# First attention of a two-layer decoder block: transposed scores computed by a second product, with the row maximum as two rows of the operand stacks

## The chip, the cores and the metric

One core of a Trainium2 chip runs the whole program. The metric is the device time of one execution in microseconds. An engine here is TensorE (PE; PEld is its weight load), VectorE (DVE), ScalarE (ACT), GpSimd (POOL) or SyncE (SP), which only issues transfers.

## The reference

Two layers of gated cross attention and feed-forward over x of 4 x 512 tokens x 512, all in float32. Only the first attention concerns the change:

```python
q = _qdq(x) @ _qdq(wq).T + bq            # 16 heads of 32
k, v = jnp.split(cond @ wkv.T + bkv, 2, axis=-1)
attn = softmax(einsum('bnhd,bmhd->bhnm', q, k) * 32 ** -0.5, axis=-1)   # 512 x 512 per head
o = einsum('bhnm,bmhd->bnhd', attn, v).reshape(B, N, C)
```

4 batches of 16 heads make 64 heads of 512 queries by 512 keys. Its output o goes through an int8 step, a projection and the first mixture of experts; the second layer follows. These stages are the same in both kernels.

## The kernel before

The program is a row of stages, each with a block per engine, and the engines meet between stages. `l0_projections` (L207) writes q, k and v of the first attention to DRAM as high and low halves: a float32 number is the sum of two numbers that TensorE's float32r products keep, so a product of two such numbers is a sum of products of halves. `l0_attention` (L671) is the stage of the change, `l0_output` (L981) follows it.

**Units.** 16 groups of 4 heads (`NG`, `HG0`), each head 4 tiles of 128 queries (`QT`): `N` = 256 tiles. SP loads a group's stacks: `Qs` holds for each head the rows q high, q high, q low, q low (4 x 32 = 128 rows), `Ks` k high, low, high, low, so that one product over 128 rows is the full product of the halves. Eight loads fill them (`load_stacks`, L731). `V` holds the values' halves side by side (64 columns a head) and between each two heads a block of zeros.

**Per tile.** `scores` (L850 to L860) is one product of 512 columns into one of three banks `pS`. `maxima` (DVE, L933) takes the negated maximum over 512 keys. `exps` (ACT, L903) writes exp(score - max) to `Pr` in SBUF and sums the row (`rowsum`). `transposes` (L862) turns the 128 x 512 tile by four TensorE transposes into one of three banks `pT`. `high` (ACT, L913) copies that bank to `PTh` as high halves, `low` (DVE, L940) subtracts to get the low halves `PTl`; both read PSUM. `values` (L870) multiplies: for each of the 4 key tiles of a head two products of 512 queries, high and low, into `pO`. Two heads share `pO`, each in its own 64 rows; this is what the zeros in `V` are for.

**Per pair of heads.** `o_copy` (ACT, L921) copies `pO` to SBUF, `o_transposes` (L887) turns it back by four transposes into `pR`, and `normalise` (DVE, L947 to L964) takes the reciprocals of the row sums, adds the two halves of v and multiplies. SP stores a group's output (L769).

**Order.** Each engine runs a list written by hand, in order. `pipeline` (L40) calls, for each step, the functions of an engine in the order of its list, each for the item that lies its lag behind: in TensorE's list `(values, 9)` works on the tile nine steps back. Engines meet through semaphores: `Flag.done(n)` is the value that says item n is done, `past(n, k)` that item n - k is, `free(n)` is `past(n, 2)` and `part(n, k)` speaks of part k of an item.

```python
pipeline(pe, N, 2 * UN, [(transposes, 3), (scores, 0), (values, 9), (o_transposes, 10)])
pipeline(act, N, 2 * UN, [(high, 3), (exps, 1), (o_copy, 9)])
pipeline(dve, N, 2 * UN, [(low, 4), (maxima, 0), (normalise, 10)])
```

**POOL** has no part in the attention itself. Once per group (L822 to L844) it waits for the group's scores and then issues a store of zeros to `rows` in DRAM (16 in all), at group 1 the loads of constants and weights for the next stage (`load_constants`, L3528, and `load_weights`, L805), at groups 2 to 5 `split_weights` (L812): a high and a low half of a weight tile of 896 columns and of one of 512, and at group 6 two small scalings.

## Time and profile before

| what | us |
|---|---|
| median of 3 runs (lowest, highest) | 3174.27 (3173.81, 3181.19) |
| the profiled execution | 3173.65 |
| its span, first to last instruction | 3171.9 |
| busy TensorE, weight loads | 2922.6, 2362.8 |
| busy VectorE, ScalarE, POOL | 2342.8, 2088.9, 1369.7 |

A busy time is the sum of an engine's instructions over the span; instructions of one engine can overlap a little, so their durations can be longer than the distance between their starts. "Idle before" is the time that an engine stood still just ahead of an instruction, with what ended it. An engine waits for its own list only: idle time on an engine that is not the one the others wait for costs nothing. The names of tiles carry the stage's letter: b_ is the first attention, a_ the projections before it, c_ the stage after it, and h_ is the second layer's attention.

### The profile page before, as it was taken

How to read it: one execution, taken by the hardware profiler on the slowest of the kernel's cores; microseconds unless marked ns; L12 is line 12 of the kernel's file. 1: busy time of each engine (PE TensorE's matmuls, PEld its weight loads, DVE VectorE, ACT ScalarE, POOL GpSimd, SP SyncE). 2: the span in 40 equal slices, each digit the busy share in tenths (PEclk: the TensorE clock that was granted, in tenths of full speed). 3: DMA queues.
4: the chain of work that ended last, by engine and by line, in shares of the span. 5: the costliest groups of instructions: out<-in, count | busy, mean ns of one | idle time of the engine just before them, and what ended most of it. 6: DMA issues, size and time to landing. Idle time of an engine off the chain costs nothing. (4 is left out here: it accounts for less than half of the span.)

```text
span 3171.9 us, 56528 instructions
## 1 busy us (share of the span) xinstructions
PE 2922.6 (92%) x15414; PEld 2362.8 (74%) x15414; DVE 2342.8 (74%) x4695; ACT 2088.9 (66%) x4262; POOL 1369.7 (43%) x1701
## 2 busy tenths in 40 slices
PE   6878997887999999789999899999999999899888
PEld 5656665676888877578878688888888888688754
DVE  5679998765777668866666189988989888734377
ACT  4478987422666546466666488888888888633265
POOL 4412000413001076166666277777777777441132
PEclk9989999898999999989999999999999999999999
DMA  6897663216888589756566523322322332296400
GB/s 205 268 225 170 150 163 101 87 39 232 290 262 285 167 290 256 197 158 182 152 187 197 187 67 98 98 75 95 96 85 84 98 96 72 71 305 198 138 35 34
DMA packets 427166, 491.09 MB, mean 155 GB/s; under 512 B 53044, under 2 KB 284372, under 8 KB 426996
## 3 DMA queue, kind: packets, MB, share of 16 engines
q1 hardware_dynamic: 414036, 436.50, 46.2%
q0 software_dynamic: 12960, 52.61, 4.8%
q8 instruction: 72, 1.18, 0.2%
q14 instruction: 98, 0.80, 0.1%
HBM read 312.69 MB, written 176.31 MB: 154 GB/s over the span
## 5 line engine op out<-in xcount | busy, mean ns | idle before, releaser
L2806 POOL TENSOR_SCALAR h_probs<-h_exp,h_rowsum_inv 128x512 f32<-128x512 f32 x512 | 356.2, 696 | 278.8 <-PE h_pT L2654 262.9
L2734 DVE TENSOR_REDUCE h_neg_max<-h_scores 128x1 f32<-128x512 f32 x512 | 349.0, 682 | 144.6 <-PE h_scores L2646 144.4
L2696 ACT ACTIVATE h_exp<-h_scores,h_neg_max 128x512 f32<-128x512 f32 x512 | 355.0, 693 | 110.7 <-DVE h_neg_max L2734 100.5
L2747 DVE TENSOR_TENSOR h_probsT_lo<-h_pT,h_probsT_hi 128x512 fp32r<-128x512 f32 x512 | 347.8, 679 | 0.0
L2654 PEld LDWEIGHTS h_pT<-ident,h_probs 128*128 128x128 f32 x2048 | 255.7, 141 | 71.5 <-POOL h_probs L2806 1.8
L2654 PE MATMUL h_pT<-ident,h_probs 128*128 128x128 f32 x2048 | 307.4, 272 | 1.0 <-POOL h_probs L2806 0.8
L2705 ACT CAST h_probsT_hi<-h_pT 128x512 fp32r<-128x512 f32 x512 | 300.6, 587 | 0.9 <-PE h_pT L2654 0.9
L2922 PE MATMUL k_acc<-k_w_hi,k_cat 128*128 128x512 f32 x512 | 201.2, 393 | 11.4 <-POOL k_w_lo L3003 10.5
L2669 PE MATMUL h_pO<-h_probsT_hi,n_lo 128*128 128x512 f32 x512 | 203.3, 397 | 0.0
L2923 PE MATMUL k_acc<-k_w_lo,k_cat 128*128 128x512 f32 x512 | 200.7, 392 | 0.0
L910 ACT ACTIVATE b_probs<-b_scores,b_neg_max 128x512 f32<-128x512 f32 x256 | 179.8, 702 | 24.4 <-DVE b_neg_max L937 24.4
L937 DVE TENSOR_REDUCE b_neg_max<-b_scores 128x1 f32<-128x512 f32 x256 | 173.3, 677 | 20.8 <-PE b_scores L859 20.8
L2908 ACT CAST k_cat<-k_cat 128x512 fp32r<-128x512 bf16 x128 | 79.2, 621 | 160.5 <-PE k_acc L2923 141.7
L2505 DVE TENSOR_TENSOR g_normed<-g_pQ,g_rstd 128x512 f32<-128x512 f32 x160 | 110.2, 689 | 99.6 <-PE g_pT L2410 97.1
L2535 POOL TENSOR_TENSOR g_rstd<-g_var_eps,neg_half 128x4 f32<-128x4 f32 x160 | 171.7, 1073 | 13.4 <-POOL g_var_eps L2533 0.2
L919 ACT CAST b_probsT_hi<-b_pT 128x512 fp32r<-128x512 f32 x256 | 151.3, 591 | 34.9 <-PE b_pT L867 34.9
L944 DVE TENSOR_TENSOR b_probsT_lo<-b_pT,b_probsT_hi 128x512 fp32r<-128x512 f32 x256 | 173.4, 678 | 0.6
L867 PE MATMUL b_pT<-ident,b_probs 128*128 128x128 f32 x1024 | 162.6, 282 | 9.6 <-DVE b_probsT_lo L944 8.0
L2793 POOL TENSOR_TENSOR n_lo<-n_raw,n_hi_second 128x512 fp32r<-128x512 f32 x128 | 165.0, 1289 | 0.0
L867 PEld LDWEIGHTS b_pT<-ident,b_probs 128*128 128x128 f32 x1024 | 116.5, 142 | 64.8 <-ACT b_probs L910 46.8
L2454 ACT ACTIVATE g_out<-g_pT,head_ln_b,head_ln_w 128x512 f32<-128x512 f32 x160 | 124.4, 778 | 57.5 <-DMA lnT<-g_out 56.9
L2400 PE MATMUL g_pQ<-g_w_hi,n_hi_second 128*128 (+1 forms) x320 | 134.2, 419 | 24.5 <-POOL g_w_lo L2518 24.5
(453 smaller groups left out, 9006.7 us busy)
## 6 DMA issues: line engine op xcount, KB each, us to landing
e_w_raw<-in_w SPq DMA_DIRECT2D x24, 1792.0 KB, 8.0
lnT<-g_out SPq DMA_DIRECT2D x160, 256.0 KB, 2.4
n_raw<-lnT SPq DMA_DIRECT2D x64, 512.0 KB
e_w_raw<-in_w SPq DMA_DIRECT2D x24, 896.0 KB, 9.7
n_raw<-lnT SPq DMA_DIRECT2D x64, 256.0 KB
n_raw<-v SPq DMA_DIRECT2D x64, 256.0 KB
cat<-h_cat SPq DMA_DIRECT2D x128, 128.0 KB, 1.8
k_cat<-cat SPq DMA_DIRECT2D x128, 128.0 KB, 4.7
```

The costliest lines, as they stand in the source:

```text
L867: last = nc.tensor.transpose(pT[r % TB][:, k], Pr[:, r % 4, bass.ts(k, P)], g["ident"][:])
L910: nc.scalar.activation(Pr[:, r % 4], pS[r % SB][:], ACT.Exp, bias=nmax[:, r % 4:r % 4 + 1], accum_out=rsum[:, gb * HG0 + h, q:q + 1]).then ...
L944: nc.vector.tensor_tensor(PTl[:, h, :, bass.ts(q, P)], pT[r % TB][:], PTh[:, h, :, bass.ts(q, P)], ALU.subtract).then_inc(lo_done.sem, 1)
L2654: last = nc.tensor.transpose(pT[r % 4][:, k], Pn[:, r % 4, bass.ts(k, P)], g["ident"][:])
L2669: nc.tensor.matmul(pO[h][:], vl, PTh[:, br * HPG + h, k], start=False, stop=(k == QT - 1)).then_inc(o_mm.sem, 1)
L2696: nc.scalar.activation(Pr[:, r % 4], pS[r % 2][:], ACT.Exp, bias=nmax[:, r % 4:r % 4 + 1], accum_out=rsum[:, r % 4:r % 4 + 1]).then_inc(ex ...
L2705: nc.scalar.copy(PTh[:, br * HPG + h, :, bass.ts(q, P)], pT[r % 4][:]).then_inc(hi_done.sem, 1)
L2734: v.tensor_reduce(nmax[:, r % 4:r % 4 + 1], pS[r % 2][:], axis=AX, op=ALU.max, negate=True).then_inc(nmax_done.sem, 1)
L2747: v.tensor_tensor(PTl[:, br * HPG + h, :, bass.ts(q, P)], pT[r % 4][:], PTh[:, br * HPG + h, :, bass.ts(q, P)], ALU.subtract).then_inc(lo_ ...
L2806: nc.gpsimd.tensor_scalar(Pn[:, r % 4], Pr[:, r % 4], rinv[:, r % 4:r % 4 + 1], 1.0, ALU.mult, ALU.mult).then_inc(norm_done.sem, 1)
L2922: nc.tensor.matmul(bank[:], lhsT, Wh[:, k], start=(k == 0), stop=False)
L2923: ins = nc.tensor.matmul(bank[:], lhsT, Wl[:, k], start=False, stop=(k == CK - 1))
```

## The change

All of it is in `l0_attention`. The unit of the lists becomes a head (`NH` = 64), its work is done in two halves of two tiles (`HALF`).

- The score product now has 96 rows (low times low is left out; six loads). It serves the maximum alone: `pS` is one buffer of two banks, and VectorE takes the maxima of two query tiles in one instruction of 2 x 512 columns.
- POOL splits the four columns of negated maxima into high and low and puts them into columns 96 and 97 of `Mx` (zeros elsewhere). `max_rows` multiplies each by an identity, which yields the maxima as two rows on partitions 96 and 97 of `pMR`; ScalarE copies them under the query stack (`max_copy`). The key stack has ones in rows 96 and 97.
- `scores_t` computes the scores a second time with keys as rows: the stacks of 98 rows give score minus maximum, transposed. ScalarE's exponential of 2 x 512 columns writes the transposed probabilities to `Pr`; there are no transposes of tiles.
- The halves are made from `Pr` in SBUF: key tiles 0 and 1 high on VectorE (`high_a`) and low on POOL (`low_a`); key tiles 2 and 3 high on ScalarE (`high_b`) and low on VectorE (`low_b`). On odd heads POOL takes key tile 2 of these low halves (`low_c`).
- `V` has 65 columns a head, the last one of ones, so row 64 of `pO` is the row sum. `o_rows` multiplies 65 rows by `fold`, which adds the value halves and turns the result, per head, 33 columns for each of four query tiles. Its target `pR` is part of the bank `pMR`. `normalise` is a reciprocal of the sum column and a multiplication over 4 x 32 columns.
- POOL's side work hangs on its list: one of 64 smaller zero stores per head, the weight split one instruction a head in heads 8 to 23, the loads at head 4. POOL's list has no loop.

The diff, cut to its core (a line of "..." marks what is left out):

```diff
-    UN = HG0 * QT
-    PAIRS = HG0 // 2
-    V_LOADS = ((0, 0, 1), (2, 1, 2), (5, 3, 1))
+    HALF = QT // 2
     NG = B * H0 // HG0
-    SB, TB = 3, 3
-    N = NG * UN
+    NH = NG * HG0
+    ROUND_TRIP = 2 * HG0
+    STACK = 3 * DH0
+    DEEP = STACK + 2
+    OW = 2 * DH0 + 1
...
-        V = m.sb("v", [P, 2, QT, 3 * PAIRS, 2 * DH0], F32R)
-        Pr = m.sb("probs", [P, 4, S])
+        V = m.sb("v", [P, 2, QT, HG0, OW], F32R)
+        Pr = m.sb("probsT", [P, 2, QT, S])
...
-        pS = [m.ps(f"scores{j}", [P, S]) for j in range(SB)]
-        pT = [m.ps(f"pT{j}", [P, QT, P]) for j in range(TB)]
+        nmax = m.sb("neg_max", [P, 2, QT])
+        Mx = m.sb("max_columns", [P, 2, QT, DEEP], F32R)
+        ident_r = m.sb("ident_r", [P, P], F32R)
+        fold = m.sb("fold_parts", [OW, DH0 + 1])
+        rinv = m.sb("rowsum_inv", [P, 2, QT])
+        pS = m.ps("scores", [P, HALF, S])
+        pST = [m.ps(f"scoresT{j}", [P, HALF, S]) for j in range(2)]
         pO = m.ps("pO", [P, S])
-        pR = m.ps("pR", [P, QT, P])
+        pMR = m.ps("pMR", [P, S])
+        pR = pMR[:, 0:QT * (DH0 + 1)].rearrange("p (k c) -> p k c", k=QT)
...
-        QK_LOADS = 8
-        ZR = ROWS // NG
...
+        QK_LOADS = 6
+        ZR = ROWS // NH
...
-                for w, stack, parts in ((0, Qs, (0, 0, 1, 1)), (1, Ks, (0, 1, 0, 1))):
+                for w, stack, parts in ((0, Qs, (0, 0, 1)), (1, Ks, (0, 1, 0))):
...
-                wait(sp, s_done.sem, s_done.depth + (n - 1) * UN)
+                wait(sp, st_done.sem, (st_done.depth + (n - 1) * HG0) * HALF)
...
-                wait(sp, o_mm.sem, o_mm.depth + (n - 1) * UN)
-                for slot, head, heads in V_LOADS:
-                    sp.dma_start(V[:, r, :, slot:slot + heads].rearrange("p k s c -> p k (s c)").bitcast(F32),
-                                 t["v0"][bass.ds(tok, S), bass.ds(ch * 2 + head * 2 * DH0, heads * 2 * DH0)]
+                wait(sp, o_mm.sem, o_mm.depth + (n - 1) * HG0)
+                for h in range(HG0):
+                    sp.dma_start(V[:, r, :, h, 0:2 * DH0].bitcast(F32),
+                                 t["v0"][bass.ds(tok, S), bass.ds(ch * 2 + h * 2 * DH0, 2 * DH0)]
                                  .rearrange("(k p) c -> p k c", p=P)).then_inc(v_in[r], 16)
...
-            for b in range(2):
-                nc.gpsimd.memset(V[:, b, :, 1::3].bitcast(F32), 0.0).then_inc(v_zeroed, 1)
+            nc.gpsimd.memset(Mx[:].bitcast(F32), 0.0).then_inc(cleared, 1)
+            nc.gpsimd.memset(V[:, :, :, :, 2 * DH0:OW].bitcast(F32), 1.0).then_inc(prepared, 1)
+            nc.gpsimd.tensor_copy(ident_r[:], g["ident"][:]).then_inc(prepared, 1)
...
-            for k in range(NG):
-                pool.wait_ge(s_done.sem, s_done.depth + max(k * UN, UN // 2))
-                pool.dma_start(rows[k * ZR * D:(k + 1) * ZR * D].rearrange("(p a) -> p a", p=P), Z[:]).then_inc(z_out, 16)
-                if k == 1:
+            def split_weights(k, step):
+                if step == 0:
...
+                k, h = divmod(n, HG0)
+                pool.dma_start(rows[n * ZR * D:(n + 1) * ZR * D].rearrange("(p a) -> p a", p=P), Z[:]).then_inc(z_out, 16)
+                if k == 1 and h == 0:
...
-                    split_weights(k - 2)
-                    if k < KT:
+                    split_weights(k - 2, h)
+                    if k < KT and h == HG0 - 1:
                         load_weights(k)
...
+                pool.wait_ge(nmax_done.sem, nmax_done.done(n))
+                pool.wait_ge(mrow_mm.sem, mrow_mm.free(n))
+                nc.gpsimd.tensor_copy(Mx[:, r % 2, :, STACK], nmax[:, r % 2]).then_inc(mx_hi.sem, 1)
+                pool.wait_ge(mx_hi.sem, mx_hi.done(n))
+                nc.gpsimd.tensor_tensor(Mx[:, r % 2, :, STACK + 1], nmax[:, r % 2], Mx[:, r % 2, :, STACK],
+                                        ALU.subtract).then_inc(mx_done.sem, 1)
+
...
+                pool.wait_ge(hi_a.sem, hi_a.done(n))
+                nc.gpsimd.tensor_tensor(PTl[:, h, 0:HALF], Pr[:, r % 2, 0:HALF], PTh[:, h, 0:HALF],
+                                        ALU.subtract).then_inc(lo_a.sem, 1)
...
+                if third(r):
+                    pool.wait_ge(hi_b.sem, hi_b.done(n))
+                    nc.gpsimd.tensor_tensor(PTl[:, h, HALF], Pr[:, r % 2, HALF], PTh[:, h, HALF],
+                                            ALU.subtract).then_inc(lo_c.sem, 1)
+                if isinstance(n, int):
+                    beside(n)
+
+            pipeline(pool, NH, ROUND_TRIP, [(max_columns, 1), (low_a, 2), (low_c, 2)], NH)
...
+                    pe.wait_ge(nmax_done.sem, nmax_done.part(n - 1, 1))
+                else:
+                    pe.wait_ge(nmax_done.sem, nmax_done.part(n, 0))
+                for j in range(HALF):
+                    last = nc.tensor.matmul(pS[:, j], Qs[0:STACK, gb, h, bass.ts(half * HALF + j, P)], Ks[0:STACK, gb, h],
+                                            start=True, stop=True)
+                last.then_inc(s_done.sem, 1)
...
+                pe.wait_ge(mx_done.sem, mx_done.done(n))
+                pe.wait_ge(o_done.sem, o_done.past(n, 4))
+                for q in range(QT):
+                    last = nc.tensor.matmul(pMR[0:DEEP, bass.ts(q, P)], Mx[:, r % 2, q], ident_r[:], start=True, stop=True)
...
+                if half == 0:
+                    pe.wait_ge(mrow_done.sem, mrow_done.done(n))
+                pe.wait_ge(exp_done.sem, exp_done.part(n - 1, half))
+                for j in range(HALF):
+                    last = nc.tensor.matmul(pST[half][:, j], Ks[0:DEEP, gb, h, bass.ts(half * HALF + j, P)],
+                                            Qs[0:DEEP, gb, h], start=True, stop=True)
+                last.then_inc(st_done.sem, 1)
...
+                    pe.wait_ge(lo_a.sem, lo_a.done(n))
+                    pe.wait_ge(oT_done.sem, oT_done.past(n, 1))
+                    if h == 0:
+                        pe.wait_ge(v_in[gb], (i + 1) * 16 * HG0)
+                else:
+                    pe.wait_ge(lo_b.sem, lo_b.done(n))
+                    if third(r):
+                        pe.wait_ge(lo_c.sem, lo_c.done(i * HG0 + r // 2))
+                for k in range(half * HALF, (half + 1) * HALF):
+                    nc.tensor.matmul(pO[0:OW], V[:, gb, k, h], PTh[:, h, k], start=(k == 0), stop=False)
+                    last = nc.tensor.matmul(pO[0:OW], V[:, gb, k, h], PTl[:, h, k], start=False, stop=(k == QT - 1))
+                if half == 1:
+                    last.then_inc(o_mm.sem, 1)
...
+                pe.wait_ge(o_done.sem, o_done.past(n, 1))
...
-                    last = nc.tensor.transpose(pR[:, k], Os[:, pair_buffer(r), bass.ts(k, P)],
-                                               g["ident"][:])
+                    last = nc.tensor.matmul(pR[:, k], Os[0:OW, r % 2, bass.ts(k, P)], fold[:], start=True, stop=True)
...
-            pipeline(pe, N, 2 * UN, [(transposes, 3), (scores, 0), (values, 9), (o_transposes, 10)])
...
+            pipeline(pe, NH, ROUND_TRIP, [(half_of(scores, 0), 0), (max_rows, 1), (half_of(values, 0), 3),
+                                          (half_of(scores_t, 0), 1), (half_of(scores, 1), 0), (half_of(values, 1), 3),
+                                          (half_of(scores_t, 1), 1), (o_rows, 4)])
...
-                nc.scalar.activation(Pr[:, r % 4], pS[r % SB][:], ACT.Exp, bias=nmax[:, r % 4:r % 4 + 1],
-                                     accum_out=rsum[:, gb * HG0 + h, q:q + 1]).then_inc(exp_done.sem, 1)
...
-                nc.scalar.copy(PTh[:, h, :, bass.ts(q, P)], pT[r % TB][:]).then_inc(hi_done.sem, 1)
...
+                act.wait_ge(mrow_mm.sem, mrow_mm.done(n))
+                nc.scalar.copy(Qs[STACK:DEEP, gb, h], pMR[STACK:DEEP]).then_inc(mrow_done.sem, 1)
...
+                n, gb, h = head(i, r)
+                act.wait_ge(st_done.sem, st_done.part(n, half))
+                if half == 0:
+                    act.wait_ge(lo_a.sem, lo_a.free(n))
+                else:
+                    act.wait_ge(lo_b.sem, lo_b.free(n))
+                    if third(r):
+                        act.wait_ge(lo_c.sem, lo_c.past(i * HG0 + r // 2, 1))
+                nc.scalar.activation(Pr[:, r % 2, half * HALF:(half + 1) * HALF], pST[half][:], ACT.Exp).then_inc(exp_done.sem, 1)
...
+                act.wait_ge(exp_done.sem, exp_done.part(n, 1))
+                act.wait_ge(o_mm.sem, o_mm.past(n, 4))
+                nc.scalar.copy(PTh[:, h, HALF:], Pr[:, r % 2, HALF:]).then_inc(hi_b.sem, 1)
...
-            pipeline(act, N, 2 * UN, [(high, 3), (exps, 1), (o_copy, 9)])
+                act.wait_ge(oTr_done.sem, oTr_done.free(n))
+                nc.scalar.copy(Os[0:OW, r % 2], pO[0:OW]).then_inc(oT_done.sem, 1)
+
+            pipeline(act, NH, ROUND_TRIP, [(max_copy, 1), (high_b, 2), (lambda i, r: exps(i, r, 0), 1), (o_copy, 3),
+                                           (lambda i, r: exps(i, r, 1), 1)])
...
+                dve.wait_ge(s_done.sem, s_done.part(n, half))
+                if half == 0:
+                    dve.wait_ge(mx_done.sem, mx_done.free(n))
+                nc.vector.tensor_reduce(nmax[:, r % 2, half * HALF:(half + 1) * HALF], pS[:], axis=AX, op=ALU.max,
...
-                nc.vector.tensor_tensor(PTl[:, h, :, bass.ts(q, P)], pT[r % TB][:],
-                                        PTh[:, h, :, bass.ts(q, P)], ALU.subtract).then_inc(lo_done.sem, 1)
...
+                dve.wait_ge(exp_done.sem, exp_done.part(n, 0))
+                dve.wait_ge(o_mm.sem, o_mm.past(n, 4))
+                nc.vector.tensor_copy(PTh[:, h, 0:HALF], Pr[:, r % 2, 0:HALF]).then_inc(hi_a.sem, 1)
...
+                dve.wait_ge(hi_b.sem, hi_b.done(n))
+                k = HALF + 1 if third(r) else HALF
+                nc.vector.tensor_tensor(PTl[:, h, k:], Pr[:, r % 2, k:], PTh[:, h, k:], ALU.subtract).then_inc(lo_b.sem, 1)
...
+                dve.wait_ge(oTr_done.sem, oTr_done.done(n))
+                dve.wait_ge(o_done.sem, o_done.free(n))
+                nc.vector.reciprocal(rinv[:, r % 2], pR[:, :, DH0]).then_inc(rinv_done.sem, 1)
+                dve.wait_ge(rinv_done.sem, rinv_done.done(n))
...
+                nc.vector.tensor_tensor(O[:, gb, :, h * DH0:(h + 1) * DH0], pR[:, :, 0:DH0],
+                                        rinv[:, r % 2].unsqueeze(2).to_broadcast([P, QT, DH0]), ALU.mult).then_inc(o_done.sem, 1)
...
+            nc.vector.memset(Ks[STACK:DEEP].bitcast(F32), 1.0).then_inc(prepared, 1)
...
-            pipeline(dve, N, 2 * UN, [(low, 4), (maxima, 0), (normalise, 10)])
...
+            pipeline(dve, NH, ROUND_TRIP, [(normalise, 5), (lambda i, r: maxima(i, r, 0), 0), (low_b, 2),
+                                           (lambda i, r: maxima(i, r, 1), 0), (high_a, 1)])
```

## Rows read from the trace of the kernel before

**Rows 1.** Windows view, the attention: busy us (count) of PE, PEld, DVE, ACT, POOL; clock; DMA

```profile
167.00:543.00 376.00, 331.55 (x1920) 250.16 (x1920) 348.42 (x608) 323.37 (x800) 38.05 (x47) 0.98 0.67 161
```

**Rows 2.** Groups of instructions, 157 to 543 us: count, busy us, mean ns, idle before, releasers

```profile
L910 ACT ACTIVATE b_probs<-b_scores,b_neg_max 128x512 f32<-128x512 f32 x256 | 179.8, 702 | 24.4 <-DVE b_neg_max L937 24.4
L944 DVE TENSOR_TENSOR b_probsT_lo<-b_pT,b_probsT_hi 128x512 fp32r<-128x512 f32 x256 | 173.4, 678 | 0.6
L937 DVE TENSOR_REDUCE b_neg_max<-b_scores 128x1 f32<-128x512 f32 x256 | 173.3, 677 | 20.8 <-PE b_scores L859 20.8
L867 PE MATMUL b_pT<-ident,b_probs 128*128 128x128 f32 x1024 | 162.6, 282 | 9.6 <-DVE b_probsT_lo L944 8.0 <-ACT b_probs L910 1.3
L919 ACT CAST b_probsT_hi<-b_pT 128x512 fp32r<-128x512 f32 x256 | 151.3, 591 | 34.9 <-PE b_pT L867 34.9
...
L956 DVE RECIPROCAL b_rowsum_inv<-b_rowsum 128x8 f32<-128x8 f32 x32 | 6.0, 188 | 0.0
```

**Rows 3.** VectorE in order of time: start us, us, engine, line, operation

```profile
300.30 0.42 DVE L962 TENSOR_TENSOR b_o<-b_o_sum,b_rowsum_inv 128x256 f32<-128x256 f32 x1
300.64 0.68 DVE L944 TENSOR_TENSOR b_probsT_lo<-b_pT,b_probsT_hi 128x512 fp32r<-128x512 f32 x1
301.24 0.68 DVE L937 TENSOR_REDUCE b_neg_max<-b_scores 128x1 f32<-128x512 f32 x1
```

**Rows 4.** TensorE in order of time, same columns

```profile
300.20 0.40 PE L884 MATMUL b_pO<-b_probsT_lo,b_v 128*128 128x512 f32 x1
300.43 0.60 PE L867 MATMUL b_pT<-ident,b_probs 128*128 128x128 f32 x4
300.79 0.48 PE L859 MATMUL b_scores<-b_k_stack,b_q_stack 128*128 128x512 f32 x1
```

**Rows 5.** Other stages, prices of the new forms: tile view, groups by form, one timeline row

```profile
L2934 DVE CAST k_w_hi<-k_w_raw x32: 415/419/1518, 2764.1 to 2863.4; 128x512 fp32r<-128x512 f32 x32
...
L2938 DVE TENSOR_REDUCE k_w_gate_up<-k_w_gate_up 128x1 f32<-128x1408 f32 x12 | 19.4, 1618 | 33.4 <-DMA k_w_gate_up<-in_wguT 24.1 <-DMA k_w_gate_up<-in_wdT 9.3
...
L392 ACT CAST a_wkv_hi<-a_wkv_raw 128x1024 fp32r<-128x1024 f32 x4 | 4.2, 1044 | 4.9 <-DMA a_wkv_raw<-in_wkv0T 4.9
...
L816 POOL TENSOR_TENSOR bc_w_lo<-b_w_raw,bc_w_hi 128x896 fp32r<-128x896 f32 x4 | 8.4, 2106 | 0.3
...
L2533 POOL TENSOR_SCALAR g_var_eps<-g_sum_sq 128x4 f32<-128x4 f32 x160 | 31.4, 196 | 113.2 <-DVE g_sum_sq L2496 112.8 <-POOL g_rstd L2535 0.4
...
L824 POOL DMA_DIRECT2D rows<-b_zero x16 | 9.0, 564 | 310.3 <-PE b_scores L859 310.3
...
562.84 1.72 PE L1458 MATMUL c_pL<-bc_gate_w,c_hT 128*128 128x8 f32 x8
```

**Rows 6.** Hops between engines, timelines of stages before and after the attention

```profile
27.65 0.61 ACT L388 CAST a_ctx_hi<-a_ctxT 128x512 fp32r<-128x512 f32 x1
...
28.34 1.28 POOL L350 TENSOR_TENSOR a_ctx_lo<-a_ctxT,a_ctx_hi 128x512 fp32r<-128x512 f32 x1 [6.21 <-ACT a_ctx_hi L388]
...
546.21 0.59 PE L1431 MATMUL c_pT<-ident_half,c_q 128*128 128x128 f16 x4 [4.84 <-DVE c_q L1248]
...
546.83 0.69 ACT L1175 ACTIVATE c_oT<-c_pT,minus_half 128x512 bf16<-128x512 f16 x1 [6.24 <-PE c_pT L1431]
...
547.57 0.13 PEld L1439 LDWEIGHTS c_pY<-bc_wpT,c_oT 128*128 128x128 bf16 x2 [1.04 <-ACT c_oT L1175]
```

**Rows 7.** Two SBUF inputs on VectorE, without and with a POOL instruction beside it, timelines

```profile
550.28 0.69 DVE L1257 TENSOR_TENSOR c_x<-c_y,c_x_bias 128x512 f32<-128x512 f32 x1
...
554.09 1.21 DVE L1257 TENSOR_TENSOR c_x<-c_y,c_x_bias 128x512 f32<-128x512 f32 x1
...
553.49 1.26 POOL L1128 TENSOR_TENSOR c_x_bias<-bc_x,bc_bp 128x512 f32<-128x512 f32 x1
```

**Rows 8.** First and last scores (tile view), and the last instruction of the attention (timeline)

```profile
L859 PE MATMUL b_scores<-b_k_stack,b_q_stack x256: 473/476/797, 167.0 to 530.5; 128*128 128x512 f32 x128
...
542.20 0.42 DVE L962 TENSOR_TENSOR b_o<-b_o_sum,b_rowsum_inv 128x256 f32<-128x256 f32 x1
```

202 lines of the change are left out of this document (88 added, 114 removed).

## Prediction

> **What bounds the kernel now.** I read the windows view of the attention first. VectorE is busy 348.4 of 376 us, TensorE 331.6, ScalarE 323.4, POOL 38.1, at a granted clock of 0.98 [rows 1]: three engines are nearly full and the fourth is idle. The page's chain of waits covers only the last percents of the span and says nothing of this stage. Then the groups by line: per query tile VectorE does a maximum (677 ns) and a low half (678 ns), 256 of each, ScalarE an exponential (702) and a high half (591), TensorE four transposes of 282 [rows 2]. VectorE sat idle 20.8 us before the maxima, nearly all of it the start, and 0.6 before the low halves [rows 2], so it sets the pace: its instructions overlap and take a slot of 0.60 (0.68 from start to end) [rows 3]. On TensorE a 512-column product takes a slot of 0.23 and the four transposes 0.36 [rows 4], which makes it almost as full. The first scores start at 167.0, the last at 530.5 [rows 8]: 363.5 us for 255 steps, 1.425 per tile, **5.70 us per head** of four tiles. The attention ends at 542.62 [rows 8], 375.6 us after the first scores.
>
> **Removed, per head:** 16 transposes (4 slots of 0.36), four low halves and four high halves of 512 from PSUM, the sum over PSUM in the closing step, four accumulator reads, two of eight stack loads per group. **Added:** four more score products, four products of the maximum columns, closing products of 33 columns, a copy of two rows by 512, and two small POOL instructions. **Moved:** the low halves, partly to POOL, and POOL's zero stores and weight work, now queued behind them.
>
> **Work of each engine per head.** TensorE: 16 products of 512 columns at 0.23 [rows 4] = 3.68. Four closing products are float32 with a new weight tile each; the nearest row is eight router products of 8 columns in 1.72 us, 0.215 each [rows 5]: 0.86. The maximum columns also change weights for 128 columns of work: between the transposes' 0.36 for four [rows 4] and 0.86; I take 0.86, since they too are plain products. Sum **5.40**. VectorE: two maxima over 1024 columns; 1408 cost 1618 ns [rows 5] and 512 cost 677 [rows 2], so 1.05 ns a column, 1.21, a slot of 1.13. The low half 1.13 on even heads and 0.60 on odd, mean 0.87. The high half of 1024 is a cast between SBUF tiles, of which 512 columns took 0.42 against 0.68 from PSUM [rows 3, 5]: 0.62, with 1.13 as the upper end. Reciprocal 0.19 [rows 2], hop 0.04, multiply over 128 columns 0.42 less 0.13 = 0.29 [rows 3]: 0.52. Sum 4.27. ScalarE: SBUF copy of 1024 1.04 [rows 5], two exponentials of 1024 at about 1.1 each (0.70 plus the 0.43 that 512 columns add), two copies of 0.59 [rows 2], about 0.1 less each for overlap: 3.9. POOL: 896 columns with two inputs cost 2106 [rows 5], 512 cost 1.26 [rows 7], so 1024 cost 2.39; 1.26 more on odd heads; two small ones of 0.20 with hops of 0.08 [rows 5, 6]; one store of 0.56 [rows 5]. Even heads 3.5, odd 4.8. By work alone the stage would go from 5.70 to 5.40 and be TensorE's.
>
> **The loop that I expect to set the pace.** Every engine runs its list in order, and maxima of a head, second half, lead to the same instruction one head later by way of four engines. After it VectorE does the high half (0.62), then normalises the head five back (0.52). The product of the maximum rows waits for just that, because its bank is also the closing products' (o_done, past 4), and for POOL's two small instructions, which are ready at about the same moment. Then hop 0.05; four maximum products 3 x 0.215 + 0.27 = 0.92; hop 0.03; ScalarE's copy of two rows, 0.59, and behind it in its list the high half of the head before, 1.04, together 1.55; hop 0.05; VectorE's low half 0.87, which stands in its list ahead of the second maxima; maxima 1.13. Sum 0.62 + 0.52 + 0.05 + 0.92 + 0.03 + 1.55 + 0.05 + 0.87 + 1.13 = 5.74, **T = 5.75**. The hops are those seen between engines: TensorE to ScalarE 0.03, ScalarE to TensorE 0.05, to POOL 0.08 [rows 6]. So before, stages overlapped many tiles deep with three score banks; now one score buffer and one shared bank leave the loop only one head deep. Bounds: maximum products at the transposes' price take off 0.3 (5.45), a cast at VectorE's plain rate adds 0.51 (6.26).
>
> **POOL's stalls, S.** POOL has to be back for the next maxima within T. A quiet odd head is 4.8 plus what it is held by VectorE (0.62 + 0.60) = 6.0, the even one 4.1: it fits over two. In heads 8 to 23 it also splits weights: the 2.11 instruction [rows 5] comes on an odd head, 8.1 in all, 2.35 late; the 1.26-like one [rows 7] on the next odd head, 1.5 late; four groups: 15.4. The casts fall on even heads and hide. Two pairs of weight loads, 4 x 0.56 = 2.2. At head 4 nine loads are issued at once, 5.1, of which 3.5 don't fit. S = 21, with bounds 0 and 27. VectorE's preamble (fills, small copies) lies in the wait for the first scores, most of its 20.8 us of idle time [rows 2]; I cost it at nothing, and if that cover were gone it would be a few microseconds once. Two stack loads fewer per group, four value loads in place of three and 64 smaller zero stores in place of 16 are all issued well ahead of their use: nothing; POOL's issues are counted above.
>
> **Sum.** First maxima pair: 0.71 + 0.03 + 1.21 + 0.05 + 0.71 + 0.03 + 1.21 = 4.0. After the last one, the drain: high half, normalise, maximum rows, row copy to 2.6; exponentials behind the others' work to 6.3; high half 7.3; low halves, POOL's behind VectorE's, 9.2; products 10.3; copy 10.9; closing products 11.9; normalise **12.5**. Attention 4.0 + 63T + S + 12.5 against 375.6: the change is 63T + S - 359.1 = 362.3 + 21 - 359.1 = **+24 us**. The profiled execution took 3173.65 (span 3171.9), 0.6 below the median 3174.27, so it stands for the runs as it is; 3174.27 + 24 = **3198**. What follows the attention is untouched.
>
> **Rivals.**
> Lock (0.15): on odd heads VectorE's low half and POOL's third wake on the same signal, and both read two SBUF tiles. A VectorE sum of two SBUF tiles took 0.69 alone and 1.21 when it started 0.60 behind a POOL instruction; it ended 0.55 after POOL's end at 554.75 [rows 7], so it stood still. No row of mine shows VectorE woken by ScalarE; POOL's hop of 0.08 is the longest seen [rows 6], so I let VectorE win; if POOL wins, 1.26 every second head, T = 6.38, +64, **3238**. The Trainium skill, SBUF — State Buffer, "Who interferes with whom", has this as an exclusive lock held for the instruction, for VectorE copies in its two-port mode too; by that rule alone POOL's 2.4 us instruction can stop the high half as well, and the trace agrees for the pair above.
>
> TensorE the bound, faster (0.15): if maximum products cost what transposes do or the normalise is early, T falls to TensorE's 5.40, and POOL's extra work hides in even heads (S = 5): 340.2 + 5 - 359.1 = -14, **3160**. For it: by work VectorE and ScalarE have over 1 us to spare per head. Against: with S = 21 it needs T under 5.22 for a gain of 9.5, less than TensorE's own work; both things must go well. It decides at T = 5.37 if S = 21, 5.70 if S = 0.
>
> Even (0.18): T = 5.55, S = 10: +1, **3175**.
>
> Main case 0.52. About 0.3%, 9.5 us, is what a measurement of this kernel can tell from no change. Faster 0.15, same 0.2 (the even case and a little of the main), slower 0.65. The range: 3160 takes in the fast case's centre, 3242 the lock case's and the cast at plain rate (T = 6.26, +56).
>
> **What would show it.** Right: in the after profile the spacing of the second maxima near 5.75; TensorE idle before the maximum products with VectorE's normalise or POOL as releaser; VectorE idle before the low half, released by ScalarE; VectorE's busy time in the stage near 64 x 4.27 = 273 us, 75 less, and yet a longer stage; POOL near 4.2 us a head where it splits nothing, and the spacing worst in heads 8 to 23. Wrong: TensorE without idle time and a spacing of 5.4; high half at 1.2 us; low halves of over 1.5 us on odd heads (the lock); spacing the same in heads 8 to 23 as later (S too large); any move outside the attention.

## The result, and the profile after

The changed kernel took 3216.7 us (median of 4 runs, 3214.0 to 3218.6), the kernel before 3177.7 in the same comparison (4 runs, 3173.8 to 3185.2): ratio 1.0111, 95% interval [1.0094, 1.0128]: slower by 1.1%. The prediction said +24 us; the ratio makes it 35 (30 to 41), and the two profiled spans differ by 43.3 (3215.2 against 3171.9).

Where the time came in, by the starts and ends of tiles in the two traces. The first fence is the kernel after: three windows of the attention (columns as in [rows 1]), its last output and the tile c_so that comes behind it (tile view: min/median/max ns, first to last start). The second is the kernel before: a window at the start, and c_so.

```profile
172.00:209.00 37.00, 30.32 (x117) 20.27 (x118) 22.73 (x26) 21.07 (x25) 22.30 (x25) 0.73 0.67 137
233.00:345.00 112.00, 93.47 (x436) 65.78 (x435) 71.05 (x94) 65.00 (x79) 94.27 (x90) 0.86 0.45 116
345.00:563.00 218.00, 204.01 (x1069) 143.82 (x1068) 165.35 (x230) 160.08 (x191) 172.47 (x175) 0.98 0.49 123
...
L1025 DVE TENSOR_TENSOR b_o<-b_pMR,b_rowsum_inv x64: 290/291/292, 200.4 to 577.5; 128x128 f32<-128x128 f32 x64
...
L1311 DVE TENSOR_SCALAR c_so<-c_amax x16: 153/153/155, 583.7 to 678.6; 128x1 f32<-128x1 f32 x16
```

```profile
171.00:209.00 38.00, 29.34 (x166) 22.24 (x164) 30.36 (x53) 29.44 (x75) 6.68 (x11) 0.87 1.06 232
...
L1242 DVE TENSOR_SCALAR c_so<-c_amax x16: 153/153/154, 545.2 to 640.5; 128x1 f32<-128x1 f32 x16
```

The attention ends at 577.79 instead of 542.62 [rows 8]: +35.2, of which 1.2 is a later start. From its end to c_so it is 5.9 us instead of 2.6: +3.3. The other 4.8 lie in later stages. There the kernels below run the same code, and yet the time from c_so to the end of the span goes from 2624.3 us (e3) to 2638.4 (e9), so I give the 4.8 no cause.

VectorE is relieved as meant, from 348.4 busy of 376 us [rows 1] to 165.4 of 218 (282.4 us over the whole attention, where the prediction had 273), and no engine turns that into time: the stage is longer. In the windows TensorE's granted clock is 0.73 in the first 37 us (0.87 before), 0.86 where POOL splits weights, 0.98 in the quiet rest. Groups of after, 172 to 563 us, forms apart:

```profile
L1002 DVE TENSOR_REDUCE b_neg_max<-b_scores 128x2 f32<-128x1024 f32 x127 | 154.9, 1220 | 13.1 <-PE b_scores L904 11.1
L874 POOL TENSOR_TENSOR b_probsT_lo<-b_probsT,b_probsT_hi 128x1024 fp32r<-128x1024 f32 x62 | 147.9, 2385 | 0.0
L1009 DVE CAST b_probsT_hi<-b_probsT 128x1024 fp32r<-128x1024 f32 x62 | 42.4, 683 | 0.0
L1015 DVE TENSOR_TENSOR b_probsT_lo<-b_probsT,b_probsT_hi 128x1024 fp32r<-128x1024 f32 x31 | 42.3, 1365 | 55.8 <-ACT b_probsT_hi L984 55.8
L915 PE MATMUL b_pMR<-b_ident_r,b_max_columns 128*98 128x128 f32 x252 | 37.3, 275 | 36.2 <-POOL b_max_columns L868 25.7 <-DVE b_o L1025 9.4
L967 ACT CAST b_q_stack<-b_pMR 2x512 fp32r<-2x512 f32 x63 | 36.5, 579 | 116.7 <-PE b_pMR L915 116.7
L1015 DVE TENSOR_TENSOR b_probsT_lo<-b_probsT,b_probsT_hi 128x512 fp32r<-128x512 f32 x31 | 21.5, 692 | 41.6 <-ACT b_probsT_hi L984 41.6
```

Where [rows 2] had 0.6 us of idle time before VectorE's low halves, there are now 97, released by ScalarE's high half; ScalarE waits 116.7 us for the maximum rows, and TensorE's maximum products wait 36 for POOL and VectorE. Each waits for the next: that is the loop. One turn of it in a quiet odd head, and the next, even one (timeline of after; start us, us, engine, line, operation; only the instructions of the loop):

```profile
423.12 1.22 DVE L1002 TENSOR_REDUCE b_neg_max<-b_scores 128x2 f32<-128x1024 f32 x1
424.26 0.68 DVE L1009 CAST b_probsT_hi<-b_probsT 128x1024 fp32r<-128x1024 f32 x1
424.41 0.58 POOL L866 CAST b_max_columns<-b_neg_max 128x4 fp32r<-128x4 f32 x1 [1.92 <-DVE b_neg_max L1002]
424.86 0.17 DVE L1021 RECIPROCAL b_rowsum_inv<-b_pMR 128x4 f32<-128x4 f32 x1
425.06 0.29 DVE L1025 TENSOR_TENSOR b_o<-b_pMR,b_rowsum_inv 128x128 f32<-128x128 f32 x1
425.50 0.53 PE L915 MATMUL b_pMR<-b_ident_r,b_max_columns 128*98 128x128 f32 x4 [0.38 <-DVE b_o L1025]
426.07 0.58 ACT L967 CAST b_q_stack<-b_pMR 2x512 fp32r<-2x512 f32 x1 [1.42 <-PE b_pMR L915]
426.68 1.06 ACT L984 CAST b_probsT_hi<-b_probsT 128x1024 fp32r<-128x1024 f32 x1
427.76 0.69 DVE L1015 TENSOR_TENSOR b_probsT_lo<-b_probsT,b_probsT_hi 128x512 fp32r<-128x512 f32 x1 [1.28 <-ACT b_probsT_hi L984]
427.81 1.80 POOL L881 TENSOR_TENSOR b_probsT_lo<-b_probsT,b_probsT_hi 128x512 fp32r<-128x512 f32 x1 [0.19 <-ACT b_probsT_hi L984]
428.37 1.22 DVE L1002 TENSOR_REDUCE b_neg_max<-b_scores 128x2 f32<-128x1024 f32 x1
...
433.14 1.23 DVE L1015 TENSOR_TENSOR b_probsT_lo<-b_probsT,b_probsT_hi 128x1024 fp32r<-128x1024 f32 x1 [1.14 <-ACT b_probsT_hi L984]
434.29 1.22 DVE L1002 TENSOR_REDUCE b_neg_max<-b_scores 128x2 f32<-128x1024 f32 x1
```

From second maxima to second maxima 5.25 us with the short low half and 5.92 with the long one. The last heads repeat 5.92 and 5.24 within a hundredth: **T = 5.585**, the mean of the two. On the odd head, 423.12 to 428.37: maxima 1.14, high half 0.60, normalise to its end 0.49, to the start of the maximum products 0.15, these 0.57, row copy 0.61, high half of ScalarE with its hop 1.08, low half 0.61; sum 5.25.

And one stall, in a head in which POOL takes the 896-column subtraction (timeline of after):

```profile
243.34 0.68 DVE L1009 CAST b_probsT_hi<-b_probsT 128x1024 fp32r<-128x1024 f32 x1
243.39 0.75 POOL L845 DMA_DIRECT2D rows<-b_zero  x1
...
244.16 2.09 POOL L821 TENSOR_TENSOR bc_w_lo<-b_w_raw,bc_w_hi 128x896 fp32r<-128x896 f32 x1
...
246.18 0.20 POOL L866 CAST b_max_columns<-b_neg_max 128x4 fp32r<-128x4 f32 x1
...
246.80 0.89 PE L915 MATMUL b_pMR<-b_ident_r,b_max_columns 128*98 128x128 f32 x4 [2.32 <-POOL b_max_columns L868]
...
248.34 0.63 PE L942 MATMUL b_pO<-b_probsT_hi,b_v 128*65 128x512 f32 x1
248.77 0.63 PE L943 MATMUL b_pO<-b_probsT_lo,b_v 128*65 128x512 f32 x1
...
249.41 1.29 DVE L1015 TENSOR_TENSOR b_probsT_lo<-b_probsT,b_probsT_hi 128x1024 fp32r<-128x1024 f32 x1 [3.68 <-ACT b_probsT_hi L984]
```

The maxima were there at 243.4, POOL comes for them at 246.18. TensorE stands still for 2.32 us, and then its 512-column products take slots of 0.43 instead of 0.23, the lower of its two clock levels. The spacing of that head was 8.61, 2.7 more than a quiet one of its kind.

### The profile page after: what moved, and what is told of

Its sections match the earlier page's. It is cut to its first block and busy times, and to the rows that moved or that the text cites. A ratio compares the mean times of both kernels' runs of the same rounds, so it can differ in the third digit from the quotient of the medians.

```text
span 3215.2 us, 55302 instructions
## 1 busy us (share of the span) xinstructions
PE 2959.2 (92%) x15286; PEld 2369.8 (74%) x15286; DVE 2284.5 (71%) x4476; ACT 2034.9 (63%) x3782; POOL 1653.5 (51%) x1974
## 5 line engine op out<-in xcount | busy, mean ns | idle before, releaser
L1002 DVE TENSOR_REDUCE b_neg_max<-b_scores 128x2 f32<-128x1024 f32 x128 | 156.2, 1220 | 17.9 <-PE b_scores L904 16.0
L2862 POOL TENSOR_TENSOR n_lo<-n_raw,n_hi_first 128x512 fp32r<-128x512 f32 x120 | 155.3, 1294 | 0.0
L874 POOL TENSOR_TENSOR b_probsT_lo<-b_probsT,b_probsT_hi 128x1024 fp32r<-128x1024 f32 x64 | 152.7, 2386 | 1.4 <-DVE b_probsT_hi L1009 1.4
L2511 ACT ACTIVATE g_squares<-g_pQ 128x512 f32<-128x512 f32 x160 | 95.5, 597 | 71.8 <-PE g_pQ L2469 66.3
L978 ACT ACTIVATE b_probsT<-b_scoresT 128x1024 f32<-128x1024 f32 x128 | 131.3, 1026 | 13.9 <-PE b_scoresT L924 12.6
L1015 DVE TENSOR_TENSOR b_probsT_lo<-b_probsT,b_probsT_hi 128x1024 fp32r<-128x1024 f32 x64 | 66.3, 1036 | 101.0 <-ACT b_probsT_hi L984 101.0
```

Of the source, the lines that this page charges most:

```text
L1002: nc.vector.tensor_reduce(nmax[:, r % 2, half * HALF:(half + 1) * HALF], pS[:], axis=AX, op=ALU.max, negate=True).then_inc(nmax_done.sem, 1)
L2862: nc.gpsimd.tensor_tensor(Lo[:, gb, slot], Raw[:, gb, slot], Hi[gb][:, slot], ALU.subtract).then_inc(op_lo.sem, 1)
```

## The experiments

Each is one edit of the kernel after, except where said. Four theories stood against each other: the **loop** through four engines; **TensorE's own work**; the SBUF **port** that VectorE and POOL share (also the long POOL instruction as such); and the granted **clock**, which by this theory falls when TensorE is held up. Spacings are differences of the starts of second maxima in each trace; "heads 8 to 23" are the 16 spacings that end with these heads. After, e4 (6 runs) and e8 (4) were run more than once, every other kernel here once. Since the stages behind the attention, with the same code, differ by up to 14 us, I read a kernel by its attention (first scores to last output) and not by its total alone. The pause is the time from there to c_so.

| kernel | time, us | attention | heads 8 to 23, mean | last 28 spacings, mean | pause |
|---|---|---|---|---|---|
| before | 3177.7 | 375.6 | | | 2.6 |
| after | 3216.7 | 409.6 | 6.98 | 5.60 | 5.9 |
| e1 | 3244.6 | 440.5 | 7.32 | 6.25 | 5.5 |
| e14 | 3212.5 | 409.8 | 7.02 | 5.60 | 5.9 |
| e12 | 3333.8 | 530.7 | 8.39 | 8.04 | 2.3 |
| e13 | 3246.4 | 435.6 | 7.40 | 6.00 | 5.9 |
| e10 | 3214.3 | 407.0 | 7.03 | 5.60 | 5.9 |
| e2 | 3198.3 | 392.9 | 6.54 | 5.47 | 5.9 |
| e11 | 3178.9 | 374.1 | 5.63 | 5.47 | 5.6 |
| e3 | 3249.0 | 449.6 | 7.44 | 6.32 | 3.9 |
| e9 | 3212.5 | 396.2 | 6.38 | 5.60 | 7.9 |
| e5 | 3202.1 | 398.8 | 6.66 | 5.56 | 2.3 |
| e4 | 3202.2 | 400.2 | 6.10 | 5.94 | 2.3 |
| e8 | 3172.4 | 369.4 | 5.51 | 5.47 | 2.3 |

**e1: without the products of the low halves.**

```diff
-  nc.tensor.matmul(pO[0:OW], V[:, gb, k, h], PTl[:, h, k], start=False, stop=(k == QT - 1))
```

> The changed kernel without the four products of a head that multiply the low halves of the probabilities (they are left out of the result; the halves are still made). Measured in the changed kernel: a head takes 5.59 us in its steady part, spacing of the second maxima 5.92 and 5.24 in turn. TensorE's work per head falls from about 4.96 us to 4.04 (4 x 0.23). Theory loop: four engines in a circle set the pace and these products are not on it: 5.59 stays, within 0.1. Theory TensorE: its work sets the pace: 4.7. Theory port: VectorE and POOL exclude each other at SBUF and their sum sets the pace: 5.59 stays.

Measured 3244.6 us, 28 more than after, with four products a head fewer. The last heads at a full clock are spaced as in after (5.24, 5.92), so TensorE's work sets nothing there; but others take 7.5 to 7.7. The windows view of the quiet heads, and rows of TensorE and VectorE inside them:

```profile
349.00:590.00 241.00, 218.88 (x914) 154.60 (x913) 166.49 (x228) 157.04 (x191) 172.23 (x175) 0.78 0.44 110
...
422.90 1.75 PE L951 MATMUL b_pMR<-b_fold_parts,b_oT 65*128 65x33 f32 x8
...
424.69 0.18 DVE L1020 RECIPROCAL b_rowsum_inv<-b_pMR 128x4 f32<-128x4 f32 x1 [1.43 <-PE b_pMR L951]
...
427.09 1.22 PE L924 MATMUL b_scoresT<-b_q_stack,b_k_stack 98*128 98x512 f32 x2
...
429.46 0.63 PE L924 MATMUL b_scoresT<-b_q_stack,b_k_stack 98*128 98x512 f32 x2
```

Two products in 1.22 us, then the same two in 0.63: the clock changes level in the middle of a head, 0.78 on average. At the lower level the closing products take 1.75 instead of 0.98, VectorE's normalise waits 1.43 for them, and so the clock gets into the loop.

**e14: the high products twice.** The control for e1: the products of the low halves become a repeat of those of the high halves.

```diff
-  PTl[:, h, k], start=False, stop=(k == QT - 1))
+  PTh[:, h, k], start=False, stop=(k == QT - 1))
```

> The kernel after with each product of a low half replaced by the same product of the high half once more (left out: the products of the low halves, as in e1; every wait stays). TensorE has as many products of 512 columns as in the kernel after, 16 a head, where e1 had 12. If e1 and e12 were slow only because four products of 512 columns a head were missing and the granted clock fell with them: as the kernel after, quiet heads 5.24 and 5.92 at a clock of 0.98, 3217, that is 28 us faster than e1 with more work. Rival (the clock falls since the low halves are not read, or for a reason in the other engines): as e1, clock 0.8, 3240 or more.

Measured 3212.5, spacings 5.25 and 5.91 as in after, and the clock back:

```profile
345.00:563.00 218.00, 204.45 (x1073) 144.12 (x1072) 164.80 (x230) 160.53 (x193) 173.57 (x175) 0.98 0.49 123
```

Four more 512-column products a head make the kernel 32 us faster than e1. That e1 was slower through the clock is shown: with the products back the clock is back (0.98 against 0.78), and the waits above say how a low clock costs time.

**e12: e1, with the closing products twice.**

```diff
-  for k in range(QT):
+  for k in [*range(QT), *range(QT)]:
       last = nc.tensor.matmul(pR[:, k], Os[0:OW, r % 2, bass.ts(k, P)], fold[:], ...)
```

> e1 (the products of the low halves left out) with every closing product issued twice into the same place: eight more products a head, 0.98 us by the slot of 0.12, so that TensorE has 5.14 us a head where e1 had 4.16 and the kernel after 5.08. Clock theory (e1 was slower since TensorE, with less to do, idled and was granted a lower clock, 0.78 in the quiet heads): with more work the clock comes back above 0.9 and the kernel is faster than e1 in spite of it; the doubled products end about 0.5 us later on the loop, so 5.6 to 6.1 a head: 3215 to 3240. Rival (something else slows e1, and the clock is only low beside it): the added work costs what it takes, 63 x 0.5 to 0.98 = 31 to 62 us more than e1, 3275 or more.

Measured 3333.8, 89 more than e1. The clock theory's forecast failed; the rival's total ("or more") holds, but its sum doesn't: the clock went from 0.78 to 0.65, and the cost was more than the added work's 31 to 62. TensorE is busy 284 of 293 us by the profile and yet slow:

```profile
345.00:638.00 293.00, 283.95 (x1172) 217.29 (x1172) 166.86 (x220) 153.75 (x184) 169.96 (x170) 0.65 0.39 94
```

So "TensorE idles" was too simple a cause for the clock: here it fell with TensorE full (at 449.52 two products take 1.21 instead of 0.63, with no idle time over 0.3 us in the head before). What the clock follows is left open.

**e13: the maximum products twice.**

```diff
-  for q in range(QT):
+  for q in [*range(QT), *range(QT)]:
       last = nc.tensor.matmul(pMR[0:DEEP, bass.ts(q, P)], Mx[:, r % 2, q], ident_r[:], ...)
```

> The kernel after with the four products of the maximum columns issued twice, 0.42 us more a head in the place that the prediction's sum took too dear (0.92, measured 0.57 with its hop). Loop theory: every microsecond there is on the loop, quiet heads from 5.58 to 6.0, +27 us, 3243. TensorE theory (its work, 5.08 to 5.5, lies under 5.58): quiet heads unchanged, 3217. Clock theory on top: TensorE's idle share stays, so the clock should stay at 0.98 in the quiet heads.

Measured 3246.4. Eight products take 0.88 where four took 0.53, and the quiet heads go to 5.60 and 6.26, mean 5.93, +0.35: exactly what was added, at an unchanged clock. The maximum products lie on the loop. A bound by TensorE's total would give the same number here; it is e1's last heads that rule that out.

```profile
427.85 0.88 PE L915 MATMUL b_pMR<-b_ident_r,b_max_columns 128*98 128x128 f32 x8 [0.48 <-DVE b_o L1025]
...
355.00:587.00 232.00, 218.04 (x1217) 157.56 (x1216) 164.61 (x229) 159.12 (x191) 171.76 (x175) 0.98 0.47 115
```

**e10: POOL's low half on one of its two tiles.**

```diff
-  nc.gpsimd.tensor_tensor(PTl[:, h, 0:HALF], Pr[:, r % 2, 0:HALF], PTh[:, h, 0:HALF], ...)
+  nc.gpsimd.tensor_tensor(PTl[:, h, 0:1], Pr[:, r % 2, 0:1], PTh[:, h, 0:1], ...)
```

> The kernel after, but POOL's first low half covers one of its two tiles (left out: the low part of every second key tile, which stays zero); the instruction falls from 2.39 to about 1.25 us, TensorE's, ScalarE's and VectorE's instructions are all the same. Loop theory (POOL's low half is not on the loop): the quiet heads stay at 5.59; heads 8 to 23 gain what POOL has less to do, to about 6.2; 3203. Port theory (POOL's long instructions hold VectorE's high half and low half): quiet heads at 5.24 to 5.3, the measured spacing of the heads in which nothing collides; heads 8 to 23 about 5.9; about 30 us less than the kernel after, 3187.

Measured 3214.3. POOL is busy 129 of 216 us instead of 172 of 218, and the quiet heads stay at 5.24 and 5.91. The port theory falls for them. Heads 8 to 23 did not gain either (7.03 after 6.98, where the loop theory had 6.2), so in this loop their loss isn't set by POOL's total. The trace shows why a shorter first low half is no help there: POOL's second one waits for ScalarE's high half in any case, 1.30 us now (236.48) instead of 0.19 (241.64 in after), and the weight work comes behind it.

```profile
340.00:556.00 216.00, 202.45 (x1063) 142.93 (x1062) 163.08 (x228) 158.82 (x191) 128.96 (x175) 0.98 0.50 124
```

**e2: ScalarE's high half ahead of the row copy.**

```diff
-  [(max_copy, 1), (high_b, 2), (lambda i, r: exps(i, r, 0), 1), ...
+  [(high_b, 2), (max_copy, 1), (lambda i, r: exps(i, r, 0), 1), ...
```

> ScalarE's list with the high half of the head before (high_b, 1.05 us) ahead of the copy of the two maximum rows instead of behind it. ScalarE waits 1.4 us for those rows, so the high half fits into that wait. Theory loop: 1.0 us leaves the circle, the spacing falls from 5.59 to TensorE's work and what it waits for, about 5.1. Theory port: VectorE's low half can start earlier but stands still until POOL's instruction of 2.39 us is through, so it takes well over 1.23 in the records and the spacing stays at 5.4 to 5.6. Theory TensorE: 5.59 stays.

Measured 3198.3: 18 us less than after, 16.7 of it in the attention. The last heads settle near 5.5 and 5.4, clock 1.00, not at the loop theory's 5.1. Now POOL's low half does hold VectorE's: an even one takes 1.71 instead of 1.23.

```profile
430.81 1.71 DVE L1015 TENSOR_TENSOR b_probsT_lo<-b_probsT,b_probsT_hi 128x1024 fp32r<-128x1024 f32 x1
...
339.00:547.00 208.00, 200.79 (x1064) 139.56 (x1063) 189.27 (x228) 158.84 (x191) 171.94 (x174) 1.00 0.52 129
```

**e11: e2 with e10's half low half.** No more in the diff than these two.

> e2 (high half ahead of the row copy) with the first low half of POOL on one of two tiles as in e10 (the same part left out). With the loop shorter and the port relieved only TensorE's own work is left: 16 slots of 0.23, 0.42 and 0.98, 5.08 us. Port theory: e2's 5.49 falls to 5.1 to 5.2, quiet heads at a clock of 1.00, heads 8 to 23 about 5.6, 3165. Rival (e2's 5.49 is another loop, over scores and maxima, in which POOL has no part): 5.45 to 5.5 as in e2, gain in heads 8 to 23 alone, 3188.

Measured 3178.9; the quiet heads 5.47 against 5.49 in e2, so the port doesn't set e2's pace either: the rival's number for the quiet heads was right. VectorE's even low half is back at 1.22 (431.68), but the maxima behind it then wait 0.29 for TensorE's scores (433.18). TensorE is busy 201.75 of 208 us there. The last thing it waits for is again the normalise, which frees the bank of the maximum products; no run tests what sets the 5.47:

```profile
428.99 0.98 PE L953 MATMUL b_pMR<-b_fold_parts,b_oT 65*128 65x33 f32 x8
...
430.00 0.18 DVE L1022 RECIPROCAL b_rowsum_inv<-b_pMR 128x4 f32<-128x4 f32 x1 [0.37 <-PE b_pMR L953]
430.22 0.29 DVE L1026 TENSOR_TENSOR b_o<-b_pMR,b_rowsum_inv 128x128 f32<-128x128 f32 x1
...
430.66 0.53 PE L916 MATMUL b_pMR<-b_ident_r,b_max_columns 128*98 128x128 f32 x4 [0.16 <-DVE b_o L1026]
```

Heads 8 to 23 fell from 6.54 (e2) to 5.63: here, without the old loop, the room that POOL has does count.

**e3: normalise, then high half at once, at the head of VectorE's list.**

```diff
-  [(normalise, 5), (maxima 0, 0), (low_b, 2), (maxima 1, 0), (high_a, 1)]
+  [(normalise, 5), (high_a, 2), (maxima 0, 0), (low_b, 2), (maxima 1, 0)]
```

> VectorE's list with the high half (high_a, 0.62 us) behind the normalise instead of ahead of it. Theory loop: the copy of the maximum to its rows no longer waits for the high half; 0.6 us leaves the circle at its start, spacing about 5.0 to 5.1, then TensorE. Theory port: POOL's low half of 2.39 us starts as late as before, VectorE's low half now becomes ready while it runs and is held until its end; spacing no better than 5.4. Theory TensorE: 5.59 stays.

Measured 3249.0, 32 more than after, against the loop theory's 5.0 to 5.1 a head. POOL's low half starts later since the high half does; its second one runs into the next maxima, the maximum products wait 0.79 for POOL's columns at 475.56, and the clock is 0.90 in the quiet heads. Shortening one arc of the loop lengthened another. Here the port does take part, as its theory said: VectorE's short low half, ready while POOL's of 2.41 runs (from 469.89), takes 1.24 instead of 0.69, and where POOL splits weights VectorE's high half stands still for a whole POOL instruction:

```profile
279.43 2.75 DVE L1009 CAST b_probsT_hi<-b_probsT 128x1024 fp32r<-128x1024 f32 x1
279.54 2.08 POOL L821 TENSOR_TENSOR bc_w_lo<-b_w_raw,bc_w_hi 128x896 fp32r<-128x896 f32 x1
...
471.61 1.24 DVE L1015 TENSOR_TENSOR b_probsT_lo<-b_probsT,b_probsT_hi 128x512 fp32r<-128x512 f32 x1 [0.67 <-ACT b_probsT_hi L984]
```

**e9: low parts of the weights filled with zeros.**

```diff
-  nc.gpsimd.tensor_tensor(shared.a_low[:, k], Ar[:, k % 2], shared.a_high[:, k], ...)
+  nc.gpsimd.memset(shared.a_low[:, k].bitcast(F32), 0.0)          (c_low in the same way)
```

> The kernel after, but POOL fills the expert weights' low parts with zeros in place of computing them (left out: the low parts of the expert weights). It sizes the term S of heads 8 to 23. Prediction's reckoning (the two subtractions of a group cost 2.35 and 1.5 us): heads 8 to 23 from 6.98 to about 6.0 per head, 15 us less in all, 3201. Clock theory (the stalls also lower TensorE's clock, to 0.86 there, and that costs as much again): heads 8 to 23 down to 5.6 to 5.7, a clock of 0.95 or more, 21 us less, 3195. Rival (the stalls are the casts' and loads', or of the zero stores): over 6.5, less than 8 us.

Measured 3212.5, but the attention ended 13.3 us earlier than in after (heads 8 to 23 at 6.38, clock 0.95 from 226 to 330 us), near the prediction's reckoning of 15. Two thirds of it did not reach the end of this single run: 2.0 went in the pause, the rest in later stages, and why is open.

**e5: zero stores on SP.**

```diff
   def load(i, r):                       # SP
+      sp.wait_ge(zeroed, 1)
+      for h in range(HG0): sp.dma_start(<zero rows of head h>, Z[:]).then_inc(z_out, 16)
   def beside(n):                        # POOL
-      pool.dma_start(rows[n * ZR * D:(n + 1) * ZR * D]..., Z[:]).then_inc(z_out, 16)
```

> The kernel after with the 64 zero stores issued by SP instead of POOL, 0.56 to 0.76 us less on POOL per head, the weight work where it was. Loop theory with S from POOL's stalls: quiet heads stay at 5.58 (0.06 less on even heads at most), heads 8 to 23 and head 4 gain what POOL has less to do, each stall shorter by 0.6 to 0.7: four groups of two stalls, 5 us, and half as much again where the clock falls less; 3208. Port or POOL-sum theory: quiet heads fall too, to 5.3 or less, 3195. Rival (no part): 3217.

Measured 3202.1, 15 less than after. In the quiet part the odd heads are unchanged and the even ones at 5.75 to 5.91, a little under 5.92; heads 8 to 23 are at 6.66. The attention ends 12.6 earlier (10.8 of it is its length); and the pause behind it, 5.9 in after, is 2.3, less than before's 2.6:

```profile
L1026 DVE TENSOR_TENSOR b_o<-b_pMR,b_rowsum_inv x64: 291/291/293, 199.1 to 564.9; 128x128 f32<-128x128 f32 x64
...
L1312 DVE TENSOR_SCALAR c_so<-c_amax x16: 153/154/155, 567.5 to 660.1; 128x1 f32<-128x1 f32 x16
```

POOL's last statement in the attention waits for all 64 zero stores; the change put the last of them into the last head. The end of after, the issue of that last store and the first work of the next stage:

```profile
573.39 0.57 POOL L845 DMA_DIRECT2D rows<-b_zero  x1
...
582.98 0.69 DVE L1309 TENSOR_REDUCE c_amax<-bc_o 128x1 f32<-128x512 f32 x1 [5.19 <-PEq L130]
```

By the trace the store lands 2.1 us behind its issue, so before the attention ends at 577.79. But the next stage starts 9.6 us behind the issue of POOL's last store in after, e1, e2, e3, e10, e11, e13 and e14 alike, however long the rest of the attention takes (hence pauses from 3.9 to 5.9). In e9 the last store takes 4.0 to land and the distance is 11.5: both times about 7.5 us from landing to the next stage. In e12 the rest takes longer than that, and the pause is 2.3, as in e4, e5 and e8 with the stores on SP. That POOL's late store causes the pause is shown; what fills the 7.5 us behind its landing is open.

**e4: e5, and POOL's other side work in smaller pieces**: splits one per even head, the 896-column one in two parts, the nine loads of head 4 spread.

```diff
+  if n % 2: return
+  if n in (4, 6): load_weights((n - 4) // 2)
+  if 8 <= n < 8 + 2 * 5 * KT: wk, step = divmod((n - 8) // 2, 5); split_weights(wk, step)
```

> POOL's side work taken out of its way: the zero stores are issued by SP, the weight split is on even heads only from head 8 to 46 with its longest instruction in two parts, the loads of constants come late and spread. Theory: the first third of the stage is slow because POOL's list is too long there; heads 8 to 23, now at 7.07 us a head on average, fall to 5.6, and of the 39 us that the stage has over 63 x 5.59 no more than 8 are left: about 31 us less than the changed kernel, 3186, a tie with the kernel before. The steady part stays at 5.59 if the loop sets it, falls by up to 0.5 if POOL's stores (0.56 to 0.76 each) count in the port's sum. Rival: the slow first third comes from the loads of stacks and values or from the clock; then it stays and the time with it.

Measured 3202.2 (6 runs), ratio to before 1.0069 [1.0047, 1.0090], short of the expected 3186. Heads 8 to 23 go to 6.10 and not to 5.6, but the pieces now last until head 47, and in after's loop each costs something: heads behind the 25th have a mean of 5.98 at a clock of 0.95. Spread over twice as many heads, half the gain comes back as a loss.

**e8: e2 and e4 together.**

> ScalarE's high half ahead of its row copy, and POOL's side work as in e4 (zero stores on SP, weight pieces one per even head). Port theory (VectorE and POOL keep each other from SBUF, and POOL's total work counts): the high half first brought 5.49 us per head in the quiet heads, the side work took heads 8 to 23 from 6.98 to 6.10; together about 5.6 in the heads with a piece and 5.5 elsewhere, attention near 378, 3180 us, no different from the kernel before. Sum theory (the two savings simply add, -20 and -15 of 3217): 3182. Clock theory (every stall that goes also lets TensorE's clock come back): below 5.4 per head all through, 3165. Loop theory of the prediction alone (POOL plays no part once the row copy is out of the way): 5.1 to 5.2, 3155.

Measured 3172.4 us (4 runs, 3170.5 to 3173.2), ratio to the kernel before 0.9957 [0.9940, 0.9974]: **faster than both kernels**, by 0.4% against the kernel before, and between what the clock theory (3165) and the port theory (3180) had. The heads from the fourth on are at 5.1 to 5.6, but two of 6.2; the clock is 1.00 from 210 us on:

```profile
210.00:522.00 312.00, 301.77 (x1594) 209.13 (x1593) 278.09 (x343) 238.46 (x285) 275.66 (x233) 1.00 0.58 142
```

The two edits save 44 us together where apart they saved 18 and 15 (in the attention 40 against 17 and 9). Once ScalarE's high half comes first, a piece of weight work in an even head hides. TensorE, busy 97% of the stretch, looks like the nearest bound, but no run tests that.

## Why the prediction was right, and where it was off

**The loop: right.** Its stations, their order and the waits stand in the trace as the text had them, and for the quiet heads e1's last heads rule out TensorE's work, e10 the port, and e2 and e13 move the pace by changing the loop. T came out at 5.585 instead of 5.75, 10 us less over 63 heads. **The term that failed in it is the maximum products**: taken at 0.92 and a hop of 0.03 from the router products, measured 0.57 with the hop, about the lower bound, what transposes cost: -0.38. The row was misread, too: its eight entries are four products (`route` makes four a tile, the trace shows 128 entries for 16 tiles), 0.43 each and not 0.215, and a closing product also stands as two entries, the four as x8 in 0.98. The maximum products, on float32r operands, are one entry each, as the transposes are, and that was the row to take. Three small things gave 0.26 back: the hop from VectorE to TensorE was 0.15 and not 0.05, row copy and high half took 1.69 with their hop in place of 1.60, and even heads wait for POOL's columns (5.92 - 5.25 is 0.67, the two low halves differ by 0.54; half of the rest is 0.07). High half and normalise were 0.05 shorter: 5.74 - 0.38 + 0.26 - 0.05 = 5.57. High half 683 ns, maxima 1220, closing step 180 and 291, long POOL low half 2385: as predicted.

**POOL's stalls: the cause right in the main, the size not.** The 63 spacings sum to 390.6; less 63 x 5.585 that is S = 39 instead of 21, beyond the upper bound of 27. Reading the list of spacings against the quiet 5.24 and 5.92: the four 896-column subtractions 10.5 (predicted 9.4); the four subtractions of the second weight with the two pairs of loads 13.0 (8.2); head 4's nine loads 5.0 (3.5); casts, held to be hidden, 4.3; the fold of the gates 1.3; the first three heads 4.2 (0). Three things were missing. One is the clock: a stall is followed by products in slots of 0.43, as after 246.80 above; the stretch has 0.86, the start 0.73. The text gave TensorE one price per product throughout, from rows at a clock of 0.98. The second is the port in the stalled heads: VectorE's low half took 2.16 instead of 1.23 at 264.75, beside a POOL cast of 896 columns, and again 2.17 at 295.02; and POOL waits 0.58 for its own subtraction before it issues the next loads (260.46). The third is the start: the loads were put at nothing, but in the first spacing, 8.02, TensorE waits 3.45 for the key stack of heads 1 to 3 (175.44), as the kernel before does (5.60 at 177.37). How the excess divides among them no run shows.

**Start and end.** First pair 5.0 (4.0; each pair of score products took 1.22 there, at the lower clock, instead of 0.71), drain 13.9 (12.5). With T and S: 399.8 predicted for the attention - 10.4 + 17.8 + 1.0 + 1.4 = 409.6, which is 577.8 - 168.2. The two large errors had opposite signs, so the forecast landed nearer than its terms: that part is luck.

**"Any move outside the attention" would be wrong, it said, and there was one**: the +3.3 behind the end (e5). The zero stores were counted as POOL's time and not as something that the end of the stage waits for.

**Rivals.** TensorE as the bound: out (e1); by slots it has 16 x 0.23 = 3.68, 0.37 for the maximum products (425.50 to 425.87) and at most 0.98 for the closing ones, 5.03 a head. The lock: it exists, but in the quiet heads VectorE won the tie, as taken: its low half started at 427.76, POOL's at 427.81, and POOL's took 1.80 instead of 1.28. The rule of the Trainium skill (SBUF — State Buffer, "Who interferes with whom") that a two-port copy of VectorE shuts POOL out as well is borne out on POOL's side: its four-column cast, 0.20 alone, took 0.58 beside the high half (424.41), and a zero store 0.75 (243.39) instead of 0.56. The cast costs the loop nothing, since the normalise ends later; the store is why even heads wait for POOL's columns, 0.07 a head on average. The prediction's worry, a POOL instruction that stops VectorE's high half, never comes true in after (all 64 take 0.66 to 0.72), but it does in e3 (2.75, above).

## What to carry to other kernels

Where each engine has a list in a fixed order, add up the loop that leads from an instruction through the others back to the same instruction one step later, before counting work: here relief on the fullest engine gave nothing, and swapping two entries in another engine's list gave 18 us. Look at side work on an engine that was idle before as at a latency in that loop, and take it in small pieces on the steps that have room. And a stall that holds TensorE up has a second price, the lower clock behind it, so cost it with rows at that clock too.

## What the runs showed of the hardware that was not expected

- Leaving out products made the kernel slower: 12 products of 512 columns a head instead of 16, granted clock 0.78 instead of 0.98, 28 us more (e1); with 16 again 0.98 (e14). Doubling the closing products instead (16 entries of 33 columns in the trace and not 8) took it to 0.65 with TensorE 97% busy (e12).
- Small products are cheap where they follow each other: four of 128 columns with new weights take a slot of 0.37 in all (425.50 to 425.87 in after), eight entries of 33 columns 0.98, and doubling four maximum products added 0.35 (e13).
- POOL's DMA issue, 0.56, takes 0.75 when VectorE's cast between SBUF tiles runs beside it, but 0.56 beside its subtraction of two SBUF tiles (after, 433.09 and 433.14).
- The next stage starts about 7.5 us behind the landing of a store that POOL issued late, where the end of the stage waits for it (after: landed 2.1 behind its issue, next stage 9.6 behind it; e9: 4.0 and 11.5).
